# Halved weight loads, with their casts shared between VectorE and ScalarE, in a fused gated-attention and feed-forward kernel

## The reference, cut to what matters

```python
def block(x):                        # x [4096, 1024] per core
    xn = layernorm(x)
    # gated slot attention, 4 heads, K = V = 256, 64 slots per head
    q = silu(xn @ Wq); k = silu(xn @ Wk); v = xn @ Wv
    f = log_sigmoid(xn @ Wf) / 8;  s = 1 - exp(f)
    for t in tokens:                 # recurrence over tokens, per head
        hk = hk * exp(f_t) + outer(k_t, s_t)
        p  = softmax((q_t / 16) @ hk)
        hv = hv * exp(f_t) + outer(s_t, v_t)
        o_t = p @ hv
    attn = (rms_norm(o) * g_norm_w) @ Wo
    # feed-forward with a token shift
    xp = shift_by_one_token(xn)
    r  = sigmoid((mu_r * xn + (1 - mu_r) * xp) @ W_r.T)
    kk = relu((mu_k * xn + (1 - mu_k) * xp) @ W_k.T) ** 2
    return x + attn + r * (kk @ W_v.T)
```

## Time and profile before

| | us |
|---|---|
| median of 3 runs | 1935.78 |
| runs | 1933.62, 1935.78, 1973.04 |
| the profiled execution's own time | 1934.87 |
| its span, slowest core (core 4) | 1933.3 |
| spans of the 8 cores | 1927.0 to 1933.3 |
| mean granted TensorE clock of core 4, as a share of 2.4 GHz | 0.752 |

### The profile page before, as it was taken

How to read it: one execution, slowest core, us unless ns; L and a number is a source line. 1 busy time by engine, 2 the same in 40 slices (tenths; PEclk the granted TensorE clock), 3 DMA queues, 4 the chain that set the end, 5 groups by cost and what they waited for, 6 DMA issues and landing times.

```text
span 1933.3 us, 23022 instructions; the slowest of 8 cores (1927.0 to 1933.3 us)
## 1 busy us (share of the span) xinstructions
PE 1290.7 (67%) x8172; PEld 780.1 (40%) x8172; DVE 811.3 (42%) x1857; ACT 525.6 (27%) x1201; POOL 43.4 (2%) x80
## 2 busy tenths in 40 slices
PE   2406585867759586775958677595867759586774
PEld 1203352534435253443525344352534435253442
DVE  2334534354353435434343543434344353434433
ACT  1102332323223232322323232232323223232322
POOL 0000000000000000000000000000000000000000
PEclk9757695967869586785958678595867859586786
DMA  5870000000000000000000000000000000000000
GB/s 178 251 229 23 22 5 29 12 23 22 23 12 12 32 12 23 23 23 12 12 33 12 23 22 23 11 12 34 12 23 22 23 13 12 32 12 22 23 1 22
DMA packets 19136, 65.77 MB, mean 34 GB/s; under 512 B 2256, under 2 KB 3664, under 8 KB 19024
## 3 DMA queue, kind: packets, MB, share of 16 engines
q0 software_dynamic: 12736, 47.19, 6.9%
q1 hardware_dynamic: 6288, 17.12, 2.8%
HBM read 47.52 MB, written 16.78 MB: 33 GB/s over the span
## 4 chain that ended last, share of the span: by engine, by line
PE 51%; DVE 22%; ACT 11%; issue 8%; DMA 5%; DVEq 1%; SPq 0%; ACTq 0%; POOL 0%; POOLq 0%
PE pB L167 17%; PE pA L167 14%; PE pC L167 8%; PE pF L167 4%; DVE hv L826 3%; PE pT L172 2%; PE pD L167 2%; PE pE L167 2%; DVE lnscr L299 2%; ACT xn_bf L884 2%; ACT t_l L659 2%; DVE xn_bf L338 1%; DVE Bm_sb L707 1%; DVE tmp L562 1%; DVE hv_bf L831 1%
## 5 line engine op out<-in xcount | busy, mean ns | idle before, releaser
L491 DVE CAST l_hi<-t_l 128x512 bf16<-128x512 f32 x16 | 6.8, 427 | 364.8 <-ACT t_l L487 364.8
L659 ACT ACTIVATE t_l<-t_e,t_linv 128x64 f32<-128x64 f32 x128 | 34.1, 336 | 421.1 <-DVE t_linv L642 405.6
L167 PE MATMUL pC<-wo_sb,xn_bf 128*128 128x512 bf16 x256 | 111.4, 613 | 28.2 <-ACT xn_bf L884 28.2
L167 PE MATMUL pA<-wrt_sb,fstage 128*128 128x512 bf16 x256 | 62.0, 386 | 65.8 <-DVE xtail L458 65.8
L172 PE MATMUL pT<-identb_sb,xn_bf 128*128 128x128 bf16 x256 | 32.4, 305 | 92.5 <-DVE xnT L362 66.7
L167 PE MATMUL pD<-v_sb,spp 128*64 128x256 bf16 x64 | 19.6, 410 | 96.8 <-ACT o_bf L798 96.8
L903 DVE TENSOR_TENSOR ob<-pC,fstage 128x512 f32<-128x512 f32 x32 | 22.1, 692 | 136.1 <-PE pC L167 136.1
L167 PE MATMUL pA<-wvt_sb,xnT 128*128 128x512 bf16 x256 | 60.4, 378 | 25.4 <-DVE xnT L518 16.7
L884 ACT COPY xn_bf<-pT 128x512 bf16<-128x512 bf16 x64 | 34.4, 589 | 157.7 <-PE pT L172 157.7
L167 PE MATMUL pA<-xnT,wq_sb 128*128 128x256 bf16 x512 | 62.7, 277 | 19.2 <-DVE wq_sb L260 13.7
L167 PE MATMUL pF<-wo_sb,xn_bf 128*128 128x512 bf16 x256 | 74.6, 443 | 0.0
(11 more groups left out here) (162 smaller groups left out, 2643.4 us busy)
## 6 DMA issues: line engine op xcount, KB each, us to landing
out<-ob POOLq DMA_DIRECT2D x32, 512.0 KB, 2.9
xb<-x POOLq DMA_DIRECT2D x30, 512.0 KB, 4.5
stage<-wq POOLq DMA_DIRECT2D x2, 1024.0 KB, 8.6
fstage<-wq SPq DMA_DIRECT2D x2, 1024.0 KB, 8.7
fstage<-wk SPq DMA_DIRECT2D x2, 1024.0 KB, 6.9
stage<-wk POOLq DMA_DIRECT2D x2, 1024.0 KB, 6.0
fstage<-wv SPq DMA_DIRECT2D x2, 1024.0 KB, 6.3
stage<-wv POOLq DMA_DIRECT2D x2, 1024.0 KB, 6.8
```

What stands on the lines that cost most here:

```text
L167: e.matmul(out=o, lhsT=l, rhs=r, start=st, stop=sp),
L491: em("vector", lambda e: e.tensor_copy(out=l_hi[:], in_=t_l[:]), waits=[("S", l_all), ("T", scT_free[0])])
L659: em("scalar", lambda e, h=h: e.activation(out=sm_e[:, h * 64:(h + 1) * 64], in_=sm_lg[:, h * 64:(h + 1) * 64], func=AF.Exp, scale=SCALE, ...
```

## The change

Every 1 MB weight load but that of `wf` is split into two DMAs of 512 KB, one for each of the two blocks of 128 rows in the staging buffer, issued one behind the other on the same queue. Each half has its own semaphore: `WIN` and `WIN3` on SP, `WIN2` and `WIN4` on POOL. The casts change with the kind of weight:

- `wq`, `wk`, `wv`, `wrt`, `wkt` (20 loads): VectorE casts the first half and ScalarE the second, each waiting for its own half.
- `wo` (4 loads): still two VectorE instructions per load, but the first now waits for its half alone.
- `wvt` (4 loads) and `wf`: one VectorE instruction as before, for `wvt` with a wait for both halves.

`cast_val[n]` becomes a list of semaphore values, of V and, for the 20 shared loads, of S. `issue_wdma(n)` waits for all of them before it issues the first half of load n, and the matmuls that read a weight wait for all of them too. The casts on ScalarE are emitted where `need_weight` is called, which puts them into ScalarE's list at that place.

```diff
--- before.py
+++ after.py
@@ -139,7 +139,8 @@
         pT = ps("pT", [128, 1024], BF16)
         pT2 = ps("pT2", [128, 1024], BF16)
 
-        sem_names = ("XIN", "XIN2", "WIN", "WIN2", "WC", "OUT0", "OUT1", "T", "V", "S")
+        sem_names = ("XIN", "XIN2", "WIN", "WIN2", "WIN3", "WIN4", "WC",
+                     "OUT0", "OUT1", "T", "V", "S")
         sems = {n: es.enter_context(nc.semaphore(n)) for n in sem_names}
         blk = es.enter_context(nc.Block())
 
@@ -175,8 +176,8 @@
         if use_preload:
             em("scalar", lambda e: e.preload_act_table(AF.Exp))
 
-        def wdma(src_ap, dst_ap, queue, waits=()):
-            sem = "WIN" if queue == "sync" else "WIN2"
+        def wdma(src_ap, dst_ap, queue, waits=(), half=0):
+            sem = {"sync": ("WIN", "WIN3"), "gpsimd": ("WIN2", "WIN4")}[queue][half]
             em(queue, lambda e, s=src_ap, d=dst_ap: e.dma_start(out=d, in_=s),
                waits=waits, inc=sem, inc_by=16)
             return (sem, val(sem))
@@ -219,14 +220,18 @@
         def issue_wdma(n):
             nm, qt = WQ[n]
             stg = fstage if n % 2 == 0 else stage2
-            waits = [("V", cast_val[n - 2])] if n - 2 >= 0 else []
+            q = "sync" if n % 2 == 0 else "gpsimd"
+            waits = list(cast_val[n - 2]) if n - 2 >= 0 else []
             if nm == "wf":
                 src = wf_d.rearrange("(i p) c -> p i c", p=128)
                 dst = stg[:].rearrange("p (i c) -> p i c", i=8)
+                wdma_val[n] = [wdma(src, dst, q, waits=waits)]
             else:
                 src = w_d[nm].rearrange("(i p) c -> p i c", p=128)[:, 2 * qt:2 * qt + 2, :]
                 dst = stg[:].rearrange("p (i c) -> p i c", i=2)
-            wdma_val[n] = wdma(src, dst, "sync" if n % 2 == 0 else "gpsimd", waits=waits)
+                wdma_val[n] = [
+                    wdma(src[:, hh:hh + 1, :], dst[:, hh:hh + 1, :], q,
+                         waits=waits if hh == 0 else (), half=hh) for hh in range(2)]
 
         issue_wdma(0)
         issue_wdma(1)
@@ -237,10 +242,10 @@
         def plan_cast(n):
             nm, qt = WQ[n]
             stg = fstage if n % 2 == 0 else stage2
-            waits = [wdma_val[n]]
             if nm == "wf":
                 em("vector", lambda e, s=stg: e.tensor_copy(out=wf_sb[:], in_=s[:]),
-                   waits=waits, inc="V")
+                   waits=[wdma_val[n][-1]], inc="V")
+                cast_val[n] = [("V", val("V"))]
             elif nm == "wo":
                 for iq in range(2):
                     i = 2 * qt + iq
@@ -249,18 +254,25 @@
                            out=w_sb["wo"][:, i * 1024:(i + 1) * 1024],
                            in0=s[:, iq * 1024:(iq + 1) * 1024],
                            scalar1=gn[:, (i % 2):(i % 2) + 1]),
-                       waits=waits + [CONSTS], inc="V")
+                       waits=[wdma_val[n][iq], CONSTS], inc="V")
+                cast_val[n] = [("V", val("V"))]
             elif nm == "wvt":
                 em("vector",
                    lambda e, s=stg, qt=qt: e.tensor_scalar_mul(
                        out=w_sb["wvt"][:, qt * 2048:(qt + 1) * 2048], in0=s[:], scalar1=0.5),
-                   waits=waits, inc="V")
+                   waits=list(wdma_val[n]), inc="V")
+                cast_val[n] = [("V", val("V"))]
             else:
                 em("vector",
                    lambda e, s=stg, nm=nm, qt=qt: e.tensor_copy(
-                       out=w_sb[nm][:, qt * 2048:(qt + 1) * 2048], in_=s[:]),
-                   waits=waits, inc="V")
-            cast_val[n] = val("V")
+                       out=w_sb[nm][:, qt * 2048: qt * 2048 + 1024], in_=s[:, 0:1024]),
+                   waits=[wdma_val[n][0]], inc="V")
+                em("scalar",
+                   lambda e, s=stg, nm=nm, qt=qt: e.copy(
+                       out=w_sb[nm][:, qt * 2048 + 1024: qt * 2048 + 2048],
+                       in_=s[:, 1024:2048]),
+                   waits=[wdma_val[n][-1]], inc="S")
+                cast_val[n] = [("V", val("V")), ("S", val("S"))]
             if n + 2 < len(WQ):
                 issue_wdma(n + 2)
 
@@ -380,7 +392,7 @@
                 for d in range(8):
                     w = []
                     if d == 0:
-                        w = [("V", wg), ("V", xnT_doneV), ("S", xnT_doneS)]
+                        w = list(wg) + [("V", xnT_doneV), ("S", xnT_doneS)]
                         if i % 2 == 0:
                             w += bank_gates(bank)
                     mm(region, w_sb[wname][:, d * 1024 + i * 128: d * 1024 + i * 128 + 128],
@@ -410,7 +422,7 @@
                     for d in range(8):
                         w = []
                         if d == 0:
-                            w = [("V", wg), ("V", xnT_doneV), ("S", xnT_doneS)] + bank_gates(bank)
+                            w = list(wg) + [("V", xnT_doneV), ("S", xnT_doneS)] + bank_gates(bank)
                         mm(bank[:, 0:512],
                            xnT[:, d * 256 + jj * 128: d * 256 + jj * 128 + 128],
                            w_sb["wv"][:, d * 1024 + h2 * 512: d * 1024 + h2 * 512 + 512],
@@ -440,7 +452,7 @@
             need_weight("wo"); need_weight("wrt"); need_weight("wkt")
             allw = need_weight("wvt")
             em("vector", lambda e: e.tensor_copy(out=xnprevT[:, 1:2048], in_=xnT[:, 0:2047]),
-               waits=[("V", allw), CONSTS])
+               waits=list(allw) + [CONSTS])
             em("vector", lambda e: e.tensor_copy(
                 out=xnprevT[:, 0:2048].rearrange("p (i t) -> p i t", i=8)[:, :, 0],
                 in_=xtail[:, 0:8]), waits=[("V", val("V"))])
```

## The result

| | before | after |
|---|---|---|
| median | 1934.68 (10 runs) | 1947.69 (10 runs) |
| profiled execution, its span | 1934.87, 1933.3 | 1949.86, 1948.0 |
| slowest core of the profile | core 4 | core 0 |

The ratio is 1.007, with a 95% interval of 1.006 to 1.008: slower by some 13 us, where 1946.5 was forecast.

A forecast was written before the change was run, and what follows sets the result against it. Bound: a ladder in the first 150 us, each fstage load waiting for the cast before it. SP 13.2 us late less 2.1 gained is 11.1; 1934.87 + 11.1 = 1946.0, forecast 1946.5, range 1939 to 1954.

The forecast's parts named there:

- The block: ScalarE's wk and wv casts wait behind q and k read-outs, stalling both queues; SP issues 6.5, then 13.5 us late.
- Steps A to C: Loads of wq, wk, wv: q 1.0 us early, k 6.0 late, v 11.9 late.
- the pair from idle engines: Two loads started on idle engines, at wk and wv: second lands 10.3 us after the first issue.
- my lower bound: Low case for two loads started on idle engines: about 8 us, taking 2.3 us off at wk and again at wv.
- Step D: Ladder after wv: wo, wrt and wkt casts gain 2.1 us together, leaving xtail 11.1 us late.
- the rival in which the loads catch up: From wo on, eight loads land 1.4 us faster each, cancelling the delay: 1935 us; chance 0.07.
- Which the change leaves alone: From xtail to the end of the span: 1783.5 us, claimed unchanged.
- The split: Two 512 KB DMAs back to back on one queue for one load: start paid once, cost taken as nothing.
- The rule of the Trainium skill: DMAs should be 1 MiB or more; as rival, each half pays its start, 21 us more, 1967; chance 0.04.
- The 2 us per DMA: Fixed cost of about 2.0 us per DMA; paid twice on ten split ladder loads, an estimated 20 us more.
- My own reading of the prefetch: Two back-to-back 512 KB loads on POOL paid one start of some 2 us; the later landed within 5.4 us.
- The step from 1946.0 to the forecast: Run median taken as 0.9 us above the profiled execution, turning 1946.0 into 1946.5.

The follow-up runs named there:

- E1: Changed kernel with both halves of each shared weight cast by VectorE, loads still halved: 1932.2 us, ratio 0.998.
- E3: Changed kernel with ScalarE casting its halves for wrt and wkt only, VectorE both halves for wq, wk, wv: 1936.2 us, ratio 1.000.
- E2: Changed kernel with each load one 1 MB DMA again, casts still shared by VectorE and ScalarE: 1943.6 us, ratio 1.004.
- E5: Kernel before with the last wvt cast repeated eight times on VectorE before the first token shift, a 10.6 us delay: 1947.5 us, ratio 1.006.
- E12: Kernel before with 20 tiny ScalarE copies at the head of ScalarE's list: 1933.2 us, ratio 0.999.
- E6: Kernel before with its loads halved and nothing else, VectorE casting whole quarters after both halves: 1949.6 us, ratio 1.006.
- E11: Changed kernel with 20 tiny ScalarE copies at the head of ScalarE's list: 1945.7 us, ratio 1.006.
- E8: Changed kernel with ScalarE's first two wk casts moved ahead of the q read-outs, those of wv ahead of k's: 1941.4 us, ratio 1.004.
- E9: Changed kernel where, from the first wo load, each load also waits for the first half of the other queue's previous load: 1953.8 us, ratio 1.009.
- E10: Changed kernel with all halves cast by VectorE, plus a wait for the other queue's previous first half from wo on: 1938.7 us, ratio 1.002.
- E7: Changed kernel with all casts on VectorE in halves, wvt too, each buffer half reloaded once its own half is cast: 1927.4 us, ratio 0.996.

## Why the prediction was right, and where it was not

The time was forecast as 1946.5 and came as 1947.7. The block was there as told, but it cost about half of what I took, and an effect that I had denied made up for the rest. That the number came out so close is luck.

*Steps A to C.* The mechanism is as told: order of events, both queues idle, the casts directly behind the last Silu (45.24 on core 4, 48.64 on core 0; forecast near 48.6 for core 4), SP's third quarter right after the first of them (46.35 and 49.75; forecast 49.7). That core 0 meets the forecast to 0.1 us is chance, as it was made for core 4, where q began 4.2 us earlier than before and not 1.0. E1 and E3, where VectorE has the casts of `wk` and `wv`, have no block; E2, which keeps them on ScalarE, has it. ScalarE's cast took 1.04 (1.05 taken), VectorE's 0.69 (0.65). Mis-sized was the pair from idle engines. I took 10.3 us from the first issue to the last landing, by the one case before. To the start of the cast behind it, it was 9.2 for `wk` (49.75 to 58.98) and 8.7 for `wv` (71.03 to 79.72) on core 0, 7.7 (46.35 to 54.01) and 8.7 (65.97 to 74.63) on core 4; my lower bound was 8. Against their own means before, q came 1.6 early (1.0 forecast), k 3.1 late (6.0), v 7.4 late (11.9), and the first `wo` load of `fstage` went out 8.5 late (13.2).

*Step D.* I had 2.1 us of gain on the rest of the ladder. The chain of the changed kernel, core 4, from the first `wo` load on:

```profile
80.09 5.95 DMA fstage<-wo
87.34 6.01 DMA fstage<-wo
94.64 5.15 DMA fstage<-wrt
101.35 6.46 DMA fstage<-wrt
109.38 5.93 DMA fstage<-wkt
116.88 6.81 DMA fstage<-wkt
125.26 5.78 DMA fstage<-wvt
132.81 5.80 DMA fstage<-wvt
```

Seven steps of 7.53 us, where I had 8.06 less 0.3. The transfers took 6.0 on average instead of 6.7. That is the rival in which the loads catch up, in part: on six cores steps fell to 7.1 to 7.5, on cores 0 and 1 they stayed at 8.3 and 8.1. Over the eight cores the seven steps took 52.8 us instead of 56.3, so the ladder gave back 3.5, and I had 2.1. Mean `xtail` is 4.5 us late and not 11.1: of the 6.6 us between, 4.7 had gone before the first `wo` load, in steps A to C, and 1.4 went on the ladder. That of the slowest core is 10.2 later than that of the slowest before. A sum made for one core said nothing of this spread.

*What follows `xtail`.* "Which the change leaves alone" is the step that failed: 1782.3 became 1786.9, on every core. 1.2 us of it stands at the very end, from the last `xtail` to the end of the span: 105.8 to 105.9 in all kernels with whole loads (before, E2, E5, E12), 106.9 to 107.2 in those with halved ones (after, E1, E3, E6 to E11). That halving the loads brings it, E6 shows. The profile has it in the last row of GpSimd, a DRAIN behind its last output DMA, here on core 4, before and after (ns in the middle, then the start in us):

```profile
L70 POOLq DRAIN  x1: 6272/6272/6272, 1926.8 to 1926.8; - x1
L70 POOLq DRAIN  x1: 7411/7411/7411, 1928.4 to 1928.4; - x1
```

It takes 6.27 us in the four kernels with whole loads and 7.41 in all nine with halved ones, in which GpSimd issues 14 DMAs more. By what it becomes longer, no run shows. The rest lies in single super-chunks. On core 4, the third and the fourth distance between one `xtail` and the next, by windows:

```profile
361.36:474.08 112.72, 79.88 (x514) 48.59 (x513) 48.47 (x114) 32.82 (x76) 2.14 (x4) 0.76 0.05 19
474.08:588.52 114.44, 81.46 (x515) 49.03 (x513) 48.46 (x115) 32.84 (x76) 2.14 (x4) 0.75 0.05 19
```

Same work, 1.7 us more, a lower mean granted clock and 1.6 us more of busy TensorE. In both, TensorE's clock falls twice to 0.50, which is 1.2 instead of 2.4 GHz, and the later of the two stretches is 3.4 us longer in the second row. These windows cover it from its start to its end:

```profile
444.88:461.94 17.06, 6.85 (x35) 3.66 (x36) 8.96 (x28) 5.20 (x19) 0.10 (x1) 0.50 0.08 32
557.54:578.02 20.48, 10.07 (x43) 4.73 (x44) 9.50 (x28) 5.40 (x20) 0.00 (x0) 0.50 0.07 27
```

At half the clock 3.4 us hold the work of 1.7, which is the difference. The kernel before has such a super-chunk too, its third, on cores 4 and 7 (114.53) but not on core 0 (112.87). In the changed kernel, E8, E9 and E11 it is the fourth (114.4 to 114.5) on all eight cores, whenever that core began, with a seventh of 113.7 to 113.9 where 112.8 is usual, and in E3 it is the eighth (114.4), with a tenth of 113.6. These four and E3 are the kernels with halved loads and ScalarE casts together; E2 and E6, with one of the two each, have none. But the long super-chunk does not need the two: without one or both of them it stands on single cores, in the kernel before, in E5 (the seventh of cores 1 to 3, 114.55) and in E10 (the eleventh of core 1, 114.57). What goes with the two is that every core has it, at the same place. Why, I did not find.

*The split.* I had put it at nothing. It costs something alone (E6). Where casts begin on the first half the loads come earlier, by 4.4 us of mean `xtail` in E1 against before and by 3.5 in the change against E2, but the change is 4 us slower than E2 as a whole. The rule of the Trainium skill (DMA: Bandwidth & Descriptors, section Bandwidth) on DMAs of 1 MiB or more stands better than I put it: E6, with 512 KB, is slower. The 2 us per DMA of its section Anatomy of one DMA — SWDGE (gpsimd) path was not paid in full: in the execution of E6 that was profiled the mean `xtail` is 2.4 us late, where the estimate worked out from that figure was 20. My own reading of the prefetch was a little short as well: 5.4 us is from the second DMA's own issue, and from the first issue the pair took 6.0.

*The sum.* Over the runs, the mean core lost 11.0 us. Of these the part after `xtail` is 4.6, by the profiles, which leaves 6.4 for the loads (the two profiled executions have 4.5); 1.4 more come from the wider spread of the cores, and together this is the 13 measured, within 0.6. The step from 1946.0 to the forecast has a slip of its own: with the 0.9 us that I named it gives 1946.9 and not 1946.5, and the 0.9 itself came from three runs; over ten the median of the kernel before is 0.2 below its profiled execution.

## What to carry to other kernels

Before giving work to an engine that has time, look at what stands ahead of it in that engine's list and what that waits for; a queue that waits for the new work inherits all those waits. The same casts cost 15 us more on the less busy ScalarE than on VectorE, 8.9 of them by late loads. If a load has to wait for a buffer, refill the buffer in parts as they come free (E7, 7 us faster than the kernel before) before sharing the work that frees it. A total that comes out right may hold two errors: compare it stage by stage and core by core.

## What was not expected of the hardware

- Cores with the same program and equal work differed by 11.4 us at the first `xtail` (149.15 to 160.56), against 4.5 before, at mean granted clocks of 0.750 to 0.752.
- In the changed kernel the fifth and every later distance from one `xtail` to the next is the same to 0.02 us on all eight cores, pauses included, though the cores stand 11 us apart; the first four differ by 0.1 to 0.8 us from core to core. Changes in the first 150 us move the long super-chunk: it is the third in the kernel before, the fourth in the changed one, the seventh in E5, the eighth in E3, the eleventh in E10, and it costs 1.7 us or so.
- GpSimd's DRAIN at the end of the program took 6.27 us with whole loads and 7.41 with halved ones, 1800 us after the last of these loads.
